# Splitting the next batch's x later on ScalarE and more loosely on VectorE, in a fused attention and mixture-of-depths kernel

## What is computed

```python
def _L0_attn_ref(encodings, W_attn, b_attn, W_out, b_out):
    qkv = encodings @ W_attn + b_attn
    q, k, v = jnp.split(qkv, 3, axis=-1)
    q, k, v = (to_heads(q), to_heads(k), to_heads(v))
    scores = jnp.einsum('bhki,bhqi->bhkq', k, q) / math.sqrt(HEAD)
    scores = jnp.where(mask, scores, jnp.float32(-10000.0))
    attn = jax.nn.softmax(scores, axis=2)
    combined = jnp.einsum('bhkq,bhkl->bhql', attn, v)
    return combined.transpose(0, 2, 1, 3).reshape(b, n, HIDDEN) @ W_out + b_out

def _L0_ffn_ref(hidden_states, w_router, W1, b1, W2, b2):
    scores = jnp.einsum('bsd,d->bs', hidden_states, w_router)
    top_scores, top_idx = jax.lax.top_k(scores, k)
    weights = jax.nn.sigmoid(top_scores)
    selected = jnp.take_along_axis(hidden_states, top_idx[:, :, None], axis=1)
    h = jax.nn.gelu(jnp.einsum('bkd,df->bkf', selected, W1) + b1)
    processed = jnp.einsum('bkf,fd->bkd', h, W2) + b2
    return ... hidden_states with weights * processed added at top_idx

x = _layernorm(x + _L0_attn_ref(x, ...), axis=-1)
x = _layernorm(x + _L0_ffn_ref(x, ...), axis=-1)
```

## Time and profile before

| | |
|---|---|
| median of three executions | 2547.9 us |
| the profiled execution | 2547.39 us |
| its span, first to last instruction | 2545.7 us |
| mean granted TensorE clock, of full | 0.986 |
| TensorE busy | 2463.0 us, 97% |
| VectorE busy | 1663.5 us, 65% |
| GpSimd busy | 1565.3 us, 61% |
| ScalarE busy | 1190.7 us, 47% |

### The profile page before, as it was taken

One profiled execution on the slowest core, in us unless ns is written; L12 is line 12 of the kernel. 1 busy time (PEld: TensorE's weight loads), 2 busy tenths in 40 slices (PEclk: granted clock), 3 DMA queues, 4 the chain that ended last, 5 costly groups with the idle time before them and its releaser, 6 DMA issues.

```text
span 2545.7 us, 40833 instructions
## 1 busy us (share of the span) xinstructions
PE 2463.0 (97%) x14168; PEld 1824.9 (72%) x14168; DVE 1663.5 (65%) x4230; ACT 1190.7 (47%) x2035; POOL 1565.3 (61%) x1642
## 2 busy tenths in 40 slices
PE   8999999999999999999999999997999999999998
PEld 6666676766777677667767767763688888888886
DVE  7767677677776777767777777676555544553533
ACT  3665566566566556556656566555431111111110
POOL 2878778788887788778788877786232113121311
PEclk9999999999999999999999999998999999999999
DMA  4233435335344433434434344343420001010000
GB/s 174 89 126 127 146 138 191 126 125 177 127 149 159 144 134 135 171 128 169 141 127 159 129 165 149 136 159 96 158 84 28 31 26 42 25 34 25 24 27 17
DMA packets 167502, 287.45 MB, mean 113 GB/s; under 512 B 23241, under 2 KB 58121, under 8 KB 166026
## 3 DMA queue, kind: packets, MB, share of 16 engines
q1 hardware_dynamic: 160130, 267.99, 30.0%
q0 software_dynamic: 7168, 16.85, 2.1%
HBM read 116.97 MB, written 65.11 MB: 72 GB/s over the span
## 4 chain that ended last, share of the span: by engine, by line
PE 73%; POOL 7%; ACT 4%; issue 3%; DVE 2%; DMA 1%; SPq 0%; POOLq 0%; DVEq 0%; ACTq 0%
PE PS L1525 14%; PE PS L1504 13%; PE PS L1363 8%; PE PS L1451 8%; PE PS L1417 7%; PE PS L1469 7%; PE PS L1377 6%; PE PS L1371 6%; POOL Pa L830 5%; DMA h_s<-hs 1%; PE PS L1386 1%; ACT Pm L958 1%; POOL lnrs L843 1%; ACT hs L1011 1%; ACT xb L1013 1%
## 5 line engine op out<-in xcount | busy, mean ns | idle before, releaser
L830 POOL TENSOR_TENSOR Pa<-Pa,Pm 128x512 f32<-128x512 f32 (+1 forms) x602 | 740.7, 1255 | 108.2 <-ACT Pm L958 94.8
L1451 PE MATMUL PS<-Qp,Kp 128*128 128x512 f32 (+3 forms) x1536 | 490.9, 356 | 35.6 <-ACT Pm L958 20.1
L1417 PE MATMUL PS<-Kp,Qp 128*128 128x512 f32 (+3 forms) x1536 | 490.1, 354 | 13.7 <-DVE nm L1055 7.5
L958 ACT ACTIVATE Pm<-PS 128x512 f32<-128x512 f32 (+1 forms) x643 | 358.2, 568 | 278.6 <-PE PS L1451 240.1
L1055 DVE TENSOR_REDUCE nm<-PS 128x1 f32<-128x512 f32 x512 | 345.7, 688 | 181.8 <-PE PS L1417 181.4
L830 POOL TENSOR_TENSOR Pa<-Pa,P 128x512 f32<-128x512 f32 (+1 forms) x297 | 368.2, 1264 | 55.7 <-ACT P L958 49.2
L1451 PEld LDWEIGHTS PS<-Qp,Kp 128*128 128x128 f32 x1536 | 279.6, 191 | 115.4 <-ACT Pm L958 33.8
L1417 PEld LDWEIGHTS PS<-Kp,Qp 128*128 128x128 f32 x1536 | 281.0, 192 | 112.9 <-issue 43.5
L920 ACT ACTIVATE G<-PS,b1c 128x512 f32<-128x512 f32 x128 | 88.1, 688 | 539.7 <-PE PS L1504 539.7
L1063 DVE CUSTOM_DVE_ANT_0 PS<-PS,maskA 128x384 f32<-128x384 f32 (+3 forms) x512 | 245.7, 509 | 140.4 <-PE PS L1417 139.4
L1063 DVE CUSTOM_DVE_ANT_0 PS<-PS,maskA,nm 128x384 f32<-128x384 f32 (+3 forms) x512 | 266.3, 555 | 88.4 <-PE PS L1417 83.4
(11 more groups left out here) (143 smaller groups left out, 4237.4 us busy)
## 6 DMA issues: line engine op xcount, KB each, us to landing
Qp<-nat SPq DMA_DIRECT2D x192, 256.0 KB, 2.5
Kp<-nat SPq DMA_DIRECT2D x192, 256.0 KB, 2.9
o_s<-Of SPq DMA_DIRECT2D x64, 256.0 KB, 2.1
Ot<-o_s SPq DMA_DIRECT2D x64, 256.0 KB, 3.0
xb<-in_x SPq DMA_DIRECT2D x64, 256.0 KB, 3.0
h_s<-hs SPq DMA_DIRECT2D x64, 256.0 KB, 2.4
out<-xb SPq DMA_DIRECT2D x64, 256.0 KB, 2.5
x_raw<-in_xt SPq DMA_DIRECT2D x15, 1024.0 KB, 6.0
```

Source lines behind the costliest of these rows:

```text
L830: e.tensor_tensor(to, to, probs(u, k)[:, h0:h0 + many, 0:w], ALU.add).then_inc(s["padd"], many)
L958: e.activation(probs(u, k)[:, hh[0]:hh[-1] + 1, 0:w], tile_bank(j)[:, 0:len(hh) * w].rearrange("p (h n) -> p h n", n=w), ACT.Exp).then_inc ...
L1417: ins = e.matmul(to, Qp[:, u % 4, h_, qt * P:qt * P + P], Kp[:, (2 * i + k0 // 512) % 4, h_, 0:w], start=True, stop=True)
L1451: ins = e.matmul(tile_bank(j)[:, x_ * w:x_ * w + w], Kp[:, (2 * i + k // 4) % 4, h_, k % 4 * P:k % 4 * P + P], Qp[:, u % 4, h_, 512 - w:51 ...
```

## The change

For b of 1 and above, the high parts of half 1 are issued 7 and 8 beats after the load (before 5 and 6), its low parts from 8 to 11 (before 6 to 9). The high parts of half 0 stay, its low parts are issued at 6, 8, 10 and 12 beats (before 6, 7, 8 and 9). Nothing changes for batch 0. TensorE's, GpSimd's and SyncE's instructions and their order are as before. Seven lines are added ahead of the engines' code, so line numbers are 5 to 7 up (L899 is L906, L1152 is L1157, L1363 is L1367).

```diff
         load_x = {BEATS * 8 * b - (21 if c else 30): (b, c) for b in range(1, B) for c in range(2)}
         load_x[-20] = (0, 1)
+        x_hi, x_lo = {}, {}
+        for n, (b, c) in load_x.items():
+            first = 7 if b and c else 5
+            for half in range(2):
+                x_hi[n + first + half] = b, c, half
+            for k in range(KT):
+                x_lo[n + first + 1 + (2 * k if b and not c else k)] = b, c, k
...
-                if n - 5 in load_x:
-                    split_x(*load_x[n - 5], 0)
-                if n - 6 in load_x:
-                    split_x(*load_x[n - 6], 1)
+                if n in x_hi:
+                    split_x(*x_hi[n])
...
-                for k in range(KT):
-                    if n - 6 - k in load_x:
-                        split_x(*load_x[n - 6 - k], k)
+                if n in x_lo:
+                    split_x(*x_lo[n])
```

## The result

The changed kernel takes 2580.2 us (median of four executions, 2576.9 to 2582.2), beside 2546.3 us of the kernel before on the same chips: ratio 1.0131, 95% interval 1.0117 to 1.0145. It is slower by about 34 us, where 21 were forecast; the measured time lies inside the range. The profiled executions stand at 2578.9 against 2547.4 us, 31.5 apart, with spans of 2577.1 and 2545.7.

The account below looks back on a forecast made before the run. TensorE, 97% busy, was taken to lose time only in gaps and at the lower clock. 20.0 (six batches at 3.3) + 1.9 - 1.2 = +20.7 us on 2547.4 gave a forecast of 2568.5 us, 8 in 10 range 2553 to 2587.

Parts of the forecast that it names:

- the sum had 3.3: Batches 2 to 7: each grows by 3.3 us, 2.0 from the later Q job and 1.3 from the clock.
- the term of 0.95 us: ScalarE, batches 2 to 7: the waited-for exponential starts 0.95 us earlier, so TensorE's gap of 2.88 us becomes 1.93.
- sum 3.78 + 1.63 + 2.69 = 8.10: VectorE's chain to the fourth low part: 3.78 us other steps, 1.63 first subtraction, 2.69 other three; Q job 2.0 us later.
- The rule that the prediction weighed against the mean: VectorE instructions with two SBUF inputs and GpSimd's SBUF reads exclude each other entirely: subtractions 5.0 instead of 4.3 us, +0.7 per batch.
- the 2 to 4.5 that were to show the forecast right: Sign on TensorE: a new gap of 2 to 4.5 us ahead of an L1367 matmul, released by xTl, batches 1 to 7.
- The term of 1.3: TensorE's clock behind the Q job's gap, batches 2 to 7: a slow stretch costs 1.3 us per batch, bounds 0 and 1.7.
- +1.9 for the second half: Batch 1: VectorE's later low parts delay the Q job by 1.9 us, bounds -0.3 and +3.8.
- -1.2 for the first: Batch 1: spreading the first half's low parts wins 1.2 us from small TensorE gaps, bounds 0 and -1.8.
- (A): Rival: the gain arrives, Q job finds its low parts ready, VectorE's chain ending before 1071.4; 2538 us, chance 0.06.
- (C): Rival: GpSimd adds through VectorE's whole chain, three subtractions 0.76 us dearer, full 1.7 of clock; 2584 us, chance 0.13.
- (B): Rival: no difference, subtractions near 0.68 us and a Q wait under 2 us leaving the clock up; 2547 to 2552, chance 0.10.
- The K job's wait for the first half: TensorE's K job, batches 2 to 7: the later fourth low part hides under PV products; 0, at most 0.45 x 6 = 2.7 us.

Follow-up runs that it names:

- E5: Kernel before with only the second half's second high part one beat later, low parts unmoved: 2538.7 us, ratio 0.9977.
- E6: Kernel before with the second half's two high parts one beat earlier, low parts unmoved: 2536.3 us, ratio 0.9968.
- E2: Kernel before with only the second half's part of the change, high and low parts two beats later: 2575.8 us, ratio 1.0111.
- E1: Kernel before with only the first half's part of the change, low parts two beats apart: 2545.1 us, ratio 1.0004.
- E3: Changed kernel with the second half's low parts in two beats, two in each, high parts still later: 2556.4 us, 1.0046 of the kernel before.
- E4: Changed kernel with GpSimd's additions of units 8b - 3 cut to 8 columns, leaving out most of their softmax sums: 2535.3 us, 0.9957 of the kernel before.
- E7: Kernel before with ScalarE's hs and xb one beat later for every O job: 2538.4 us, ratio 0.9970.
- E9: E6 with the second half's low parts placed around GpSimd's layer norm chain: 2535.6 us, 0.9961 of the kernel before.

## Why the prediction was right, and where it was too small

*What bounds the kernel.* Right. TensorE's gaps and the clock behind them account for the difference. Per batch the measured growth is (1529.51 - 412.44) / 5 = 223.41 against (1504.38 - 411.08) / 5 = 218.66 us, 4.75, where the sum had 3.3; six times 4.75 is 28.5 of the 31.5 us between the profiled executions, and batch 1 gives 2.6 more.

*ScalarE.* The exponential moved ahead of both high parts as worked out, and the term of 0.95 us is what E5 and E6 show (1.94 for 2.88). In the change the gap is even less, 1.65, by a step I had left out: VectorE's subtractions at 128b - 15 and 128b - 14, which the change moves away, had slowed GpSimd's power and lnnb. E2, which leaves the first half alone, has 1.10. The whole change has more because the first half's fourth low part, now at 128b - 18, falls beside the row of eight additions ahead of the chain, as a third low part where two were, and each of them makes an addition of 1.28 us last 1.7 to 1.8. The eight take 11.11 us before (first row below), 11.09 in E2, and 11.64 in the change and 11.65 in E1, which have that low part (second row, E1). In E1 another subtraction makes lnrs 0.60 us instead of 0.19, while the power and lnnb are shorter; its gap is 3.02 for 2.88. The prediction said that lnnb would be late only if an addition went; it priced VectorE's wait for GpSimd and never GpSimd's for VectorE.

```profile
1050.01 11.11 POOL L830 TENSOR_TENSOR Pa<-Pa,Pm 128x512 f32<-128x512 f32 x8 [6.58 <-ACT Pm L958]
...
1048.79 11.65 POOL L837 TENSOR_TENSOR Pa<-Pa,Pm 128x512 f32<-128x512 f32 x8 [6.58 <-ACT Pm L965]
...
1060.52 0.60 POOL L846 TENSOR_SCALAR lnrs<-lnmv 128x1 f32<-128x1 f32 x1
```

*VectorE's chain.* The mechanism is right and is what makes the loss: E2 shows that it is the second half, E3 that most of it is the place of its low parts, E4 that order and contention each have a share. The step "sum 3.78 + 1.63 + 2.69 = 8.10" was too small by 1.36 us: this is the term that was mis-sized. The subtractions cost 1.17 + 0.60 + 1.66 + 1.54 = 4.97, not 4.32, and the score 1.33, not 0.63. I had taken the score at its one undisturbed row although it too reads two SBUF operands, and had priced three of the subtractions by a mean over places with and without additions, while the chain was being moved to where GpSimd adds. The rule that the prediction weighed against the mean, of the Trainium skill (SBUF — State Buffer, section Who interferes with whom), gave 5.0 us for the four; 4.97 was measured in batch 5, and 0.60 + 0.60 + 0.61 + 0.83 = 2.64 in E4, where hardly anything is left to exclude them. That the two totals agree is in part luck: it took 0.60 and half an addition, 1.25, for each of them, and one subtraction met no addition while two cost 1.66 and 1.54. By that rule the score should have been in the sum as well. One overlap in E1 doesn't fit the words "for the whole instruction"; it stands in the last section.

TensorE reached the Q job 5.6 us after it resumed (1083.71 to the tile's end at 1089.34), as the 5.67 of the prediction. From piece 14's matmul to the Q job it was 9.36 us (1063.41 to 1072.77) and is 12.48 (1081.68 to 1094.16): 3.1 us, where 2.0 was forecast. That is the chain's 1.36 more, less the 0.28 that the first gap gave beyond 0.95. The new gap of 4.82 us is beyond the 2 to 4.5 that were to show the forecast right. The matmul of piece 14 before:

```profile
1063.41 0.39 PE L1417 MATMUL PS<-Kp,Qp 128*128 128x512 f32 x1
```

*The clock.* The stretch came back behind the new gap, as said, and longer. The term of 1.3, bounded at 1.7, was too small as well: over 8 us behind that gap the granted clock is 0.60 to 0.82 in the six batches (the two extremes are shown), which is 1.4 to 3.2 us of work lost, 2.3 on average, where one stretch before cost 1.7.

```profile
870.07:878.07 8.00, 8.00 (x34) 4.21 (x34) 2.73 (x8) 1.71 (x3) 3.26 (x4) 0.60 0.29 103
...
1317.20:1325.20 8.00, 8.00 (x42) 5.36 (x43) 4.37 (x13) 2.31 (x4) 4.90 (x5) 0.82 0.28 100
```

The batch grew by only 4.75 - 3.1 = 1.6 beyond the Q job. Part of the difference is a gap of 0.7 us ahead of an A ring piece, which four of the five batches counted have before and one has after; the rest is not accounted for.

*Batch 1.* +1.9 for the second half and -1.2 for the first: the gap on xTl grew by 1.2 (1.79 to 2.96) and the small ones stayed, 0.36 + 0.47 + 0.95 + 0.41 = 2.19 us before and 0.55 + 1.58 after. The first gap of batch 2 ends 1.36 us later (412.44 for 411.08) though it is itself 1.2 us shorter, so TensorE comes to it 2.6 us later, where +0.7 was forecast. The -1.2 had no chain behind it and was wrong; the clock behind the gap on xTl, 0.50 over 5 us for 0.66 before, had no term.

*The rivals.* (A), the gain arrives, fell by the point it named: the chain ended 10.4 us after TensorE resumed, not before 5.7. (C), contention everywhere, at 2584 us, is nearer to what was measured than the forecast itself; the truth lies between them, with one of four subtractions undisturbed and with the score, dear too, in none of its terms. (B) fell. The K job's wait for the first half, bounded at 0.45, did not show.

What stays open: why the slow stretch follows some gaps and not others of the same length. Behind the 1.94 us gaps of E5 it came in half of the batches:

```profile
1060.20:1065.20 5.00, 4.95 (x24) 4.02 (x25) 4.02 (x9) 3.86 (x7) 4.92 (x5) 1.00 0.25 95
...
1276.50:1281.50 5.00, 5.00 (x18) 4.16 (x19) 4.08 (x9) 3.28 (x6) 4.92 (x5) 0.66 0.26 99
```

Nor does the length alone order them: E1's gap of 3.21 us in batch 7 had none behind it.

```profile
1503.56 0.50 PE L1455 MATMUL PS<-Qp,Kp 128*128 128x512 f32 x1 [3.21 <-ACT P L965]
...
1503.56:1508.56 5.00, 5.00 (x27) 4.37 (x28) 4.74 (x13) 3.26 (x7) 4.92 (x5) 1.00 0.22 79
```

## What to carry to other kernels

When an instruction is moved later in a fixed order, cost not only the instruction that is freed but the last user of what is moved: count what now stands ahead of it on its engine, each with its duration at that place and not with its mean. Here the exponential came 1.2 us earlier and the Q job all the same 3.1 us later; moving high parts alone, one of them (E5) or both (E6), won 0.2 to 0.4%. And when a gap shrinks, look at who is next: E6 and E7 lost part of their gain to GpSimd's mask some 16 us later. And where VectorE and GpSimd both work from SBUF, ask for each pair which holds up which: two subtractions of 0.7 us beside a short chain of GpSimd cost the engine that waits for that chain 0.8 us together.

## What was not expected of the hardware

GpSimd's two small instructions of the layer norm chain took 1.14 and 0.66 us beside VectorE's subtractions, in E5 as before, though the subtractions were at their shortest, 0.68 us, and 0.71 and 0.27 where none ran (the change, E9):

```profile
1056.26 1.14 POOL L849 TENSOR_TENSOR lnrs<-lnrs,half 128x2 f32<-128x2 f32 x1
...
1057.50 0.66 POOL L852 TENSOR_SCALAR lnnb<-lnrs,lnmv 128x2 f32<-128x2 f32 x1
```

```profile
1056.15 0.68 DVE L1156 TENSOR_TENSOR xTl<-x_raw,xTh 128x512 fp32r<-128x512 f32 x1
```

So the price of the contention was paid by GpSimd alone there. Beside the long additions both pay: the addition of 1.28 us that a low part of 1.12 us meets in the change lasts 1.73.

```profile
1075.70 1.73 POOL L837 TENSOR_TENSOR Pa<-Pa,Pm 128x512 f32<-128x512 f32 x1
...
1077.39 1.28 POOL L837 TENSOR_TENSOR Pa<-Pa,Pm 128x512 f32<-128x512 f32 x1
```

In the rows of E5 the subtraction starts 0.1 us ahead of the power. In E1 the power starts 0.14 us ahead of the subtraction, and neither pays, in all six batches:

```profile
1061.46 0.71 POOL L850 TENSOR_TENSOR lnrs<-lnrs,half 128x2 f32<-128x2 f32 x1
```

```profile
1061.60 0.68 DVE L1157 TENSOR_TENSOR xTl<-x_raw,xTh 128x512 fp32r<-128x512 f32 x1
```

So a shift of a quarter of a microsecond decides whether the chain pays; that it is the order of the two starts that does it is what the rows suggest, and no run here moves that order alone.

Of the clock: a gap of TensorE of 1.94 us was followed by a slow stretch in some batches of one execution (0.66 over 5 us) and by none in others (1.00), while the six of 1.40 to 1.51 in E9's one profiled execution never were.
